# When the projections of batch 1 are made, in a four-layer transformer kernel on one core

## The reference, cut to what matters

```
x = x + g_msa * attention(modulate(layernorm(x), sh_msa, sc_msa))
    qkv  = x @ W_qkv                          # 128 -> 3 * 16 * 64
    attn = softmax(q @ k.T * 64 ** -0.5)      # per batch and head, 256 x 256
    out  = (attn @ v) @ W_out + b_out
x = x + g_mlp * (gelu(modulate(layernorm(x), ...) @ W1 + b1) @ W2 + b2)
...                                           # layer 1: graph attention over 20 nodes, 16 heads of 8
...                                           # layers 2 and 3: attention with 16 heads of 8
```

## Time and profile before

| | us |
|---|---|
| median of 3 runs | 500.25 (498.73 to 500.51) |
| the profiled execution | 498.17 |
| its span in the trace | 496.4 |
| TensorE busy | 410.4 (83%) |
| VectorE busy | 310.9 (63%) |
| ScalarE busy | 280.1 (56%) |
| GpSimd busy | 175.7 (35%) |

### The profile page before, as it was taken

How to read it: one execution, slowest core, us unless ns; L and a number is a source line. 1 busy time by engine, 2 the same in 40 slices (tenths; PEclk the granted TensorE clock), 3 DMA queues, 4 the chain that set the end, 5 groups by cost and what they waited for, 6 DMA issues and landing times. The chain is left out here.

```text
span 496.4 us, 9353 instructions
## 1 busy us (share of the span) xinstructions
PE 410.4 (83%) x3196; PEld 261.3 (53%) x3196; DVE 310.9 (63%) x846; ACT 280.1 (56%) x596; POOL 175.7 (35%) x226
## 2 busy tenths in 40 slices
PE   4767788898889998889988788787688889799965
PEld 4534454555546555455545455445355666666644
DVE  4656776764573455726475766867688877675621
ACT  2333344375453846346755776456568566877754
POOL 7503211331263331774379222723133322321210
PEclk9999899999999999999997989879899999999997
DMA  6860033000000000120013030001222313210000
GB/s 160 303 61 2 9 30 48 1 1 1 0 1 2 1 1 12 45 73 2 0 33 85 13 101 27 3 1 41 87 75 87 96 34 98 82 59 12 3 12 11
DMA packets 34527, 21.25 MB, mean 43 GB/s; under 512 B 22832, under 2 KB 31408, under 8 KB 34096
## 3 DMA queue, kind: packets, MB, share of 16 engines
q1 hardware_dynamic: 34480, 20.65, 16.1%
HBM read 16.97 MB, written 3.67 MB: 42 GB/s over the span
## 5 line engine op out<-in xcount | busy, mean ns | idle before, releaser
L917 ACT ACTIVATE pt<-psum 128x512 f32<-128x512 f32 (+1 forms) x192 | 106.2, 558 | 95.5 <-PE psum L1514 47.2
L1121 DVE TENSOR_REDUCE negm<-psum 128x2 f32<-128x512 f32 x128 | 84.6, 683 | 38.5 <-PE psum L1443 24.7
L703 POOL TENSOR_TENSOR pairsum<-pt 128x256 f32<-128x256 f32 x64 | 46.8, 732 | 143.6 <-ACT pt L917 140.2
L714 POOL COPY big<-mT 32x1024 bf16<-32x1024 bf16 x32 | 33.2, 1038 | 119.4 <-ACT mT L909 119.0
L1489 PE MATMUL psum<-big 128*128 128x256 bf16 (+1 forms) x256 | 50.8, 268 | 4.8 <-POOL big L714 3.7
L1118 DVE TENSOR_REDUCE negm<-psum 128x3 f32<-128x384 f32 x64 | 34.8, 554 | 15.1 <-PE psum L1449 14.4
L1509 PE MATMUL psum<-big 64*128 64x256 f32 x256 | 40.1, 404 | 2.5 <-ACT pt L917 2.4
L1162 DVE TENSOR_TENSOR oT<-psum,rden 128x256 f32<-128x256 f32 x64 | 26.5, 415 | 18.8 <-ACT rden L933 18.2
L1538 PE MATMUL psum<-pt,room 128*64 128x256 f32 x256 | 35.6, 400 | 0.0
L1412 PE MATMUL psum<-hT,pt 128*128 128x256 f32 x128 | 33.3, 396 | 1.4 <-DVE negm L1121 1.3
L1538 PE MATMUL psum<-pt,vpad 128*32 128x256 f32 (+1 forms) x512 | 32.5, 373 | 1.6 <-DVE oT L1162 1.6
(11 more groups left out here) (184 smaller groups left out, 858.9 us busy)
## 6 DMA issues: line engine op xcount, KB each, us to landing
big<-scratch SPq DMA_DIRECT2D x96, 96.0 KB
scratch<-room SPq DMA_DIRECT2D x48, 64.0 KB, 2.0
adj_s<-adj SPq DMA_DIRECT2D x16, 110.0 KB, 3.7
w0s<-w SPq DMA_DIRECT2D x1, 1536.0 KB, 8.3
w3s<-w SPq DMA_DIRECT2D x1, 1088.0 KB, 10.9
room<-wqk SPq DMA_DIRECT2D x2, 512.0 KB, 6.3
xT<-x_t SPq DMA_DIRECT2D x4, 128.0 KB, 2.2
w1s<-w SPq DMA_DIRECT2D x1, 512.0 KB, 8.9
```

What stands on the lines that cost most here:

```text
L703: nc.gpsimd.tensor_tensor(pairsum[:, u % SUM_RING, :], pt[:, pt_slot(u), 0:T], pt[:, pt_slot(u), T:2 * T], ALU.add).then_inc(pairsum_ready, 1)
L714: nc.gpsimd.tensor_copy(stacks[SHIFT_ROW:128, b % ROOMS, 0, GH * g:GH * (g + 1), :], mT[SHIFT_ROW:128, at % 2, :].unsqueeze(1).broadcast_t ...
L917: nc.scalar.activation(pt[:, pt_slot(u), 0:width], psum[:, ST_BANK + u % 2, 0:width], ACT.Exp, scale=EXP_SCALE[layer]).then_inc(pt_ready, 1)
L1121: ins = nc.vector.tensor_reduce(negm[:, g, 0:NT, j], bk.rearrange("p (q k) -> p q k", q=NT), AX_X, ALU.max, negate=True)
```

## The change

```diff
--- before.py
+++ after.py
@@ -142,6 +142,7 @@
 
 
 SCORE_TICKS = 2 * H - 1
+FILL_TICK = 8
 EDGE_TICKS = 24
 
 
@@ -163,6 +164,8 @@
         if name == "attention":
             layer, b = args
             n = ATTENTIONS.index((layer, b))
+            if n and ticks.get(("attention", *ATTENTIONS[n - 1]), 0) <= SCORE_TICKS:
+                return False
             if n >= ROOMS and ("project", *ATTENTIONS[n - ROOMS]) not in ended:
                 return False
             return ticks.get(("gv", b), 0) >= 2 if layer == 0 else ended.get(("qkv", layer, b), step) + STACK_TICKS <= step
@@ -209,7 +212,7 @@
         last = None
         for phase in HEAVY:
             if phase not in ended and (phase in ticks or (can_start(phase) and (
-                    last is None or last[0] == "gv" or ticks.get(last, 0) > SCORE_TICKS))):
+                    (phase == ("gv", 1) and ticks.get(last, 0) >= FILL_TICK) or last is None or last[0] == "gv" or ticks.get(last, 0) > SCORE_TICKS))):
                 tick(phase)
             last = phase
         extra = step % EXTRA_EVERY == 0 and any(p[:2] == ("attention", 0) for p in order[-1][0])
```

## The result

The changed kernel takes 509.64 us (median of 4 runs, 506.51 to 513.02) against 500.38 for the kernel before (498.73 to 503.82): ratio 1.0204 [1.016, 1.0248]. Timed twice more, on two chips, it stood at 1.0131 [1.0082, 1.0179] and 1.0159 [1.0105, 1.0213]. (The number in front of a bracket is the ratio to the kernel before, the bracket its 95% interval; it is not the quotient of the two medians and can differ from it by 0.1 to 0.2%.) It is slower, as forecast. The forecast was +5.7 us; the three ratios are +6.6 to +10.2 us on 500, their mean +8.2. The profiled execution took 506.51 us, +8.3 to its counterpart's 498.17.

What follows compares the result with a forecast made beforehand. TensorE, busy 83% of the span, was taken as the main bound, GpSimd at 258.3 to 271.8 us. Terms -12.1 + 13.8 - 0.9 + 3.1 + 1.3 + 0.5 gave +5.7 us on the median 500.25: 505.9 us, range 499.0 to 510.0.

Steps and rivals of the forecast that it cites:

- Term 4: Layer 1 of batch 2: TensorE's second turn of weights waits behind GpSimd's clear-and-copy block, +3.1 us (bounds 0 and 5.9).
- Term 2: Early stretch the projections enter (batch 0's attention): 25.0 us of work plus 7.0 idle against 18.21, +13.8 us.
- Term 1: Late stretch the projections leave (ticks 37 to 53): four groups at 4.3 us replace 29.33 us, -12.1 us.
- Term 3: Layer 1 of batch 1: attention a tick earlier puts TensorE work ahead of waits for GpSimd's weights, -0.9 us.
- Term 5: Layer 1 of batch 2: TensorE's clock at its lower level after another long wait, +1.3 us (0 to 2.2).
- Term 6: Attention (2, batch 3): one tick less of attention ahead of its first score, which waits for a transfer, +0.5 us.
- The holes are filled: Rival: projections fill TensorE's idle time in the early stretch, which then costs +6.8; total 499.0 us, chance 0.12.
- The block is hidden: Rival: TensorE reaches the second turn in layer 1, batch 2 late, so no block or clock cost; 501.6 us, chance 0.18.
- VectorE becomes the bound in the emptied stretch: Rival: late stretch's groups cost 4.71 us or more, saving only 10.5, clock drop full 2.2; 508.4 us or more, chance 0.15.

Runs made afterwards that it cites:

- block_early: Kernel before, with only GpSimd's clear-and-copy block for batch 3 one tick earlier, between first and second weights of layer 1, batch 2: 506.44 us, ratio 1.0155.
- block_later: Changed kernel with GpSimd's clear-and-copy block written one tick later, behind the second weights of layer 1, batch 2: 499.73 us, ratio 1.001.
- gv_only: Changed kernel with batch 1's projections still moved to tick 16, but its attention starting at tick 41 as before: 500.88 us, ratio 1.0001.
- both: Changed kernel with block_later's later block and bias_vector's bias additions on VectorE together: 501.11 us, ratio 1.0042.
- dose_short: Changed kernel with only the 1.84 us clearing part of GpSimd's block between the two weights, selector copies one tick later: first to third turn 10.27 us.
- dose_middle: Changed kernel with clearing and two of four selector copies (3.84 us) between the two weights, the rest one tick later: first to third turn 14.70 us.
- shift_only: Kernel before with batch 1's projections only one tick earlier, so attentions from batch 1 to layer 2 batch 2 start a tick earlier: 510.2 us, ratio 1.0212.
- bias_vector: Kernel before with the bias additions of layer 1, batch 2, on VectorE and not GpSimd: 500.76 us, ratio 1.0049.
- fill16: gv_only with batch 1's projections starting at tick 24 and not 16: 504.13 us, ratio 1.0101.

## Why the prediction was half right

**The sign and the mechanism held, but for the last link.** The second turn waits behind the clear-and-copy block, as Term 4 said, with the block, one shift and the product ahead of it in that order; block_early and block_later show it from both sides. The second product ends 7.8 us behind the first (266.44 to 274.22), as worked out (262.3 to 270.1). What the prediction left out is ScalarE's copy of the first turned weights, which hangs on the same shift and comes 0.3 us later.

**Term 2, right to a tenth where the clock stayed.** 32.0 us were forecast, 25.0 busy and 7.0 idle. The waits came out one by one: 1.04 us behind the first value matmul (0.95 forecast), 1.25, 0.66 and 1.03 ahead of the three pairs (1.4, 0.5, 1.2), 2.36 behind them (2.3), 0.67 between the last query/key ticks (0.6). The row of the kernel before that the 0.95 rests on is TensorE's:
```profile
79.91 1.13 PE L1422 MATMUL psum<-w0s,hT 128*128 128x512 f32 x2 [0.95 <-ACT mT L905]
```
The whole stretch in the third profiled execution of the changed kernel:
```profile
27.90:59.89 31.99, 24.96 (x129) 14.31 (x130) 15.59 (x40) 11.94 (x25) 3.79 (x5) 1.00 0.19 18
```
In the first one 1.5 us of busy time are on top (33.48): TensorE's granted clock was down from 36 to 39 us, by the small waits around the first score pair. The third execution has the same waits (1.25 us again ahead of that pair) and no drop. Windows of TensorE alone in the first execution:
```profile
34.00:36.00 2.00, 1.24 (x8) 0.93 0.10 12
36.00:38.00 2.00, 2.00 (x4) 0.50 0.00 0
38.00:40.00 2.00, 2.00 (x7) 0.72 0.00 0
```
The drop was there in six of nine profiled executions with this order of the early stretch (the changed kernel twice, block_later twice, gv_only, both), each 33.5 us long, and not in three (the changed kernel's third, dose_short, dose_middle), each 32.0. With the old order (the kernel before, shift_only, block_early, bias_vector) it was in none of four. The prediction has no term for it. That the short waits make the fall possible is argued from this; no run varied them alone. The Trainium skill (TensorE: Matmul & The Clock Gate, "What's actually happening") calls the activity window free-running and the transition run-variable; nine executions of one order, six with the fall and three without, agree.

**Term 1, too small.** -12.1 forecast, -13.8 measured: groups in the emptied stretch last 15.54 / 4 = 3.9 us, not 4.3. The four groups, TensorE alone:
```profile
73.18:77.63 4.45, 3.39 (x32) 1.00 0.04 7
77.63:81.17 3.54, 3.12 (x30) 1.00 0.96 107
81.17:85.18 4.01, 3.40 (x32) 1.00 0.22 16
85.18:88.72 3.54, 3.12 (x30) 1.00 0.87 103
```
Maxima are turned in every second group only, and a group without a turn takes 3.54 us. The three groups of the earlier trace rows all have a turn in them, so a mean taken from them was too long. Another 0.9 us came with the tick: without it (gv_only) the stretch takes 16.48 us, 12.9 less than before. With Term 2 the move nets +1.5 in the first execution and nothing in the third (31.99 - 18.21 - 13.79 = 0.0), against a forecast +1.7.

**Term 3, right.** -0.9 forecast; the offset falls by 0.7 to 0.8 from before layer 1 of batch 1 to behind it, in all three executions.

**Term 4, the step that failed, by its size.** Terms 4 and 5 forecast 3.1 of wait and 1.3 of clock for layer 1 of batch 2, 4.4 together; the place took 6.5. Term 4 was mis-sized, 3.1 for 4.1, and 1.2 us of the place had no term. In its parts, against the same kernel with the block out of the way:
- The wait. I had TensorE at the second turn at 267.09, as in the kernel before, because "what is ahead of it hardly changes" (the 0.25 us named beside it did not enter the 3.1; with it the sum is 3.4). But the 4.60 us of the earlier trace rows were wholly at the lower level. In the new order, in four executions without the second wait, the way to the second turn takes 3.9 to 4.0 us, since part of it runs at the upper one (0.67 in dose_short). The old order has 3.7 (bias_vector), 4.1 (gv_only) and 4.6 (fill16) as well, so 4.60 was the long end of what one kernel does. TensorE is there earlier, so the block costs 7.98 - 3.91 = 4.1 us and not 3.1; 0.2 of it is ScalarE's copy. What TensorE is granted on the way changes the wait that the profile shows, not the time of the turn: in the third execution of the changed kernel it is busy for 4.98 of these us and waits 2.98, and the turn comes after 7.96 all the same:
```profile
264.40:272.36 7.96, 4.98 (x22) 0.70 0.34 111
```
- The clock. Behind the second wait TensorE works at the lower level again. Windows of TensorE alone in the changed kernel, first to second and second to third turn:
```profile
266.58:274.56 7.98, 3.94 (x23) 0.58 0.38 106
274.56:282.23 7.67, 7.25 (x42) 0.77 0.13 36
```
  7.67 - 6.36 = 1.3 us, just what Term 5 said; it had been picked between 0 and 2.2, so the exact hit is luck. In dose_middle it is 2.35, so the ceiling of 2.2 that I had given it was no ceiling.
- 1.2 us that block_later loses there as well (from +3.1 to +4.2 in the table of offsets), without any second wait. A row of the changed kernel that goes with it is a wait for layer 1's mask on VectorE, which stands in every kernel with the attentions a tick earlier (shift_only too) and neither in the kernel before nor in gv_only or block_early:
```profile
257.88 0.81 PE L1703 MATMUL psum<-kbd,q1T 128*128 128x320 f32 x2 [1.42 <-DVE room L1300]
```
  The prediction had no term for it. The wait for the first weights is 0.7 us shorter in return, so the 1.42 is not the whole account of the 1.2.

Sum of the place: 4.1 + 1.3 + 1.2 = 6.6, measured 6.5.

**Term 6, too small.** +0.5 forecast. The wait for the transfer of (2, batch 3), 2.42 us before, is 3.44, 3.92 and 3.98 us in the changed kernel's three executions and 2.99 in gv_only, which keeps the tick: 0.5 to 1.6 us. One kernel's executions differ by as much there (2.96 and 4.35 in block_later).

**The rivals.** "The holes are filled" is out: 7.0 us of idle time stayed. "The block is hidden" is out. Of "VectorE becomes the bound in the emptied stretch" the price is out: it is the fullest engine there (14.66 of 15.54 us), and the groups are shorter for all that.

**What stays open.** With the block between the products the kernel is 1.3% slower than with it behind (1.0159 against 1.0025 on one chip), 6.7 us on 500; the place itself explains 5.3 (15.61 - 10.28). The rest lies behind it. Over the same matmuls, 285.85 to 365.09 us in the kernel before (79.24 us), TensorE alone in the changed kernel and in block_later:
```profile
295.41:374.69 79.28, 62.94 (x475) 0.89 0.16 44
...
290.08:367.24 77.16, 61.52 (x476) 0.91 0.16 45
```
The changed kernel's three executions take 79.3, 80.7 and 78.7 us there and block_later's two 77.2 and 79.0, on average 1.5 us less. But the executions of one kernel differ by 2 us as well, so whether the block's place has a part in it no run tells.

No kernel beat the kernel before. The best of the changed ones, gv_only, block_later and dose_short, are level with it.

## What to carry to other kernels

Shifting one stream of work by a tick against another costs little on average and much at one place: look in the new order, engine by engine, for the long instruction block that has come to stand ahead of a short one that another engine waits for, and move the block, not the stream. When pricing the wait, do not take the waiting engine's arrival from one old trace: at another granted clock it comes earlier or later (3.7 to 4.6 us here). Follow every engine whose list has an instruction behind the block, not only the one that makes the awaited result. Price the slow work behind a second long wait too: here the block that held the second turn up by 2.1 us cost 4.4, the one that held it up by 4.1 cost 5.4.

## What the hardware showed that I had not expected

- Around waits of 1.04, 1.25 and 0.76 us within some 5 us, none of them long, TensorE's granted clock fell from 1.00 to 0.50 for some 3 us (36 to 39 us in the first execution) in six executions of nine with the same waits, and the stretch was 1.5 us longer each time (33.48 against 31.99).
- The cost of a second wait does not grow evenly with its length: none at 1.84 us of block, 4.4 us (first to third turn) at 3.84, 5.3 at 5.84.
- In bias_vector one addition of two SBUF operands on VectorE took three times its usual time beside an instruction of GpSimd with two SBUF operands (L800, 1.16 us at 256.69); VectorE's timeline:
```profile
255.03 0.49 DVE L1305 TENSOR_TENSOR room<-room,bias 128x320 f32<-128x320 f32 x1
...
256.75 1.44 DVE L1305 TENSOR_TENSOR room<-room,bias 128x320 f32<-128x320 f32 x1
```
  The Trainium skill (GPSIMD Engine Reference, 1. Specifications) names contention between GpSimd and VectorE instructions with two SBUF inputs; this row agrees. The two others of its kind that overlapped a GpSimd instruction took 0.58 us, beside a copy at 253.42, and 0.49, beside the last 0.1 us of an addition at 259.95, so how often it strikes is not shown.
